# A CTR tower with two CIN layers: remainder from gathered rows, near product in halves, another order of TensorE's passes

## The reference

```python
def _cin_layer(h, h0, W, b):                       # h: (B, Hn, 64), h0: (B, 32, 64)
    Wr = W.reshape(W.shape[0], Hn, Mn)
    x = jnp.einsum('bhd,bmd,ohm->bod', h, h0, Wr) + b[None, :, None]
    return jax.nn.relu(x)
x1 = _cin_layer(h0, h0, W1, b1)                    # 128 rows out of 32 x 32 pairs
next_hidden, direct1 = x1[:, :64], x1[:, 64:]
direct2 = _cin_layer(next_hidden, h0, W2, b2)      # 128 rows out of 64 x 32 pairs
z = jnp.sum(jnp.concatenate([direct1, direct2], axis=1), axis=-1)   # 192 per sample
y = relu(relu([z, dense_ctx] @ W_top1 + b_top1) @ W_top2 + b_top2) @ W_top3
```

## Time and profile before

| | |
|---|---|
| median of three runs | 2034.1 us |
| profiled execution | 2035.26 us, its span 2033.5 us |
| mean granted TensorE clock | 0.997 |
| PE busy | 1999.9 us (98%), 7038 instructions |
| PEld busy | 1325.8 us (65%) |
| DVE busy | 1923.5 us (95%) |
| ACT busy | 1713.6 us (84%) |
| POOL busy | 1647.3 us (81%) |
| DMA | 474.16 MB, mean 233 GB/s |

### The profile page before, as it was taken

How to read it: one execution, slowest core, us unless ns; L and a number is a source line. 1 busy time by engine, 2 the same in 40 slices (tenths; PEclk the granted TensorE clock), 3 DMA queues, 4 the chain that set the end, 5 groups by cost and what they waited for, 6 DMA issues and landing times.

```text
span 2033.5 us, 24093 instructions
## 1 busy us (share of the span) xinstructions
PE 1999.9 (98%) x7038; PEld 1325.8 (65%) x7038; DVE 1923.5 (95%) x546; ACT 1713.6 (84%) x4887; POOL 1647.3 (81%) x708
## 2 busy tenths in 40 slices
PE   5999999999999999999999999999999999999999
PEld 3666666666666666666666666666666666666664
DVE  6999999999999999999999999999999999999991
ACT  4788888888888888888888888888888888888873
POOL 5898887879899998887889998788999988887520
PEclk9999999999999999999999999999999999999999
DMA  7898988988988989989989989989988989989950
GB/s 227 217 268 235 245 246 232 245 248 232 245 249 234 248 244 235 250 241 236 253 237 237 254 237 236 257 232 237 257 233 238 255 231 239 255 230 238 251 131 11
DMA packets 257782, 474.16 MB, mean 233 GB/s; under 512 B 35425, under 2 KB 52321, under 8 KB 257522
## 3 DMA queue, kind: packets, MB, share of 16 engines
q1 hardware_dynamic: 230450, 396.18, 64.5%
q0 software_dynamic: 26624, 75.52, 22.0%
q10 hardware_dynamic: 576, 0.92, 0.1%
HBM read 321.49 MB, written 16.78 MB: 166 GB/s over the span
## 4 chain that ended last, share of the span: by engine, by line
PE 90%; DMA 3%; DVE 2%; ACT 2%; issue 2%; POOL 1%; SPq 0%; DVEq 0%; POOLq 0%; ACTq 0%
PE acc L592 20%; PE acc L604 17%; PE acc L605 17%; PE acc L610 17%; PE acc L615 14%; DMA plo<-pnear 2%; DVE pnear L514 2%; PE acc L595 1%; ACT phi L789 1%; ACT x L713 1%; POOL prod L308 1%; DMA x1rep<-x 1%; PE x1p L686 0%; DMA near<-emb_rows 0%; PE acc L686 0%
## 5 line engine op out<-in xcount | busy, mean ns | idle before, releaser
L271 POOL DMA_INDIRECT gathered<-in_tables,idx x256 | 655.4, 2560 | 101.8 <-POOL idx L266 51.2
L308 POOL TENSOR_TENSOR prod<-near,h 128x2048 f32<-128x2048 f32 x126 | 582.5, 4623 | 128.5 <-PE acc L595 81.1
L604 PE MATMUL acc<-phi,w2lo 128*128 128x512 f32 x1664 | 655.2, 394 | 8.2 <-ACT phi L789 8.0
L605 PE MATMUL acc<-phi,w2hi 128*128 128x512 f32 x1664 | 654.3, 393 | 0.0
L514 DVE TENSOR_TENSOR pnear<-near,x1p 128x4096 f32<-128x4096 f32 x128 | 564.9, 4413 | 6.2 <-ACT x1p L762 3.8
L514 DVE TENSOR_TENSOR pfar<-far,x1p 128x4096 f32<-128x4096 f32 x128 | 564.9, 4413 | 0.7 <-PE acc L615 0.7
L592 PE MATMUL acc<-prod,w1T 128*128 128x512 f32 x1024 | 460.1, 592 | 1.5 <-DVE prod L489 1.5
L610 PE MATMUL acc<-plo,w2hi 128*128 128x512 f32 x1664 | 454.5, 423 | 0.0
L713 ACT ACTIVATE x<-acc,bias 128x64 f32<-128x64 f32 x1024 | 305.8, 324 | 170.6 <-PE acc L595 170.6
L519 DVE TENSOR_TENSOR plo<-pnear,phi 128x3072 fp32r<-128x3072 f32 x128 | 446.2, 3486 | 0.3 <-ACT phi L789 0.3
L519 DVE TENSOR_TENSOR plo<-pfar,phi 128x2560 fp32r<-128x2560 f32 x128 | 361.2, 2822 | 45.1 <-ACT phi L801 45.0
(11 more groups left out here) (75 smaller groups left out, 1151.3 us busy)
## 6 DMA issues: line engine op xcount, KB each, us to landing
far<-emb_rows SPq DMA_DIRECT2D x512, 256.0 KB, 4.6
near<-emb_rows SPq DMA_DIRECT2D x510, 256.0 KB
plo<-pnear POOLq DMA_DIRECT2D x128, 512.0 KB
x1rep<-x SPq DMA_DIRECT2D x255, 256.0 KB, 4.3
h<-emb_rows SPq DMA_DIRECT2D x128, 256.0 KB
emb_rows<-gathered SPq DMA_DIRECT2D x127, 128.0 KB
gathered<-in_tables,idx POOLq DMA_INDIRECT x256, 6.6
rem_a<-emb_rows SPq DMA_DIRECT2D x64, 64.0 KB
```

Of the source, the lines that this page charges most:

```text
L271: nc.gpsimd.indirect_dma_start(out=gathered[s][:, g, :], out_offset=None, in_=a["tables"], in_offset=bass.IndirectOffsetOnAxis(ap=idx[s][: ...
L308: nc.gpsimd.tensor_tensor(prod1[:, :, :], near[(u + 2) % 3][:, :, :], h0[odd][:, :].unsqueeze(1).to_broadcast([P, K1, N]), ALU.mult).then_ ...
L604: nc.tensor.matmul(acc2[s][:, :], w2lo[:, t, :], phi[:, t, :], start=(t == T_DMA), stop=False)
L605: mm = nc.tensor.matmul(acc2[s][:, :], w2hi[:, t, :], phi[:, t, :], start=False, stop=(t == T_SPLIT - 1))
```

## The change

- The remainder's factors no longer come from `emb_rows`. One is the lower half of the gathered rows as they lie, the other is the upper half, moved down 64 partitions by a DMA (`move_upper`). GpSimd multiplies 64 x 256 instead of 32 x 512. ScalarE rounds once (64 x 256), at the end of odd steps, instead of twice at the front of even ones. GpSimd's subtraction writes its own tile, and three DMAs of SyncE (`place_remainder`) put the parts in one of two `rem_parts`.
- The lookups read their indices from `idx_all` directly; `place_idx` is gone.
- `pnear` is made in two instructions of 4 tiles. ScalarE rounds tiles 2 and 3 after the first, tiles 4 to 7 after the second. The part of `plo` for the DMA has its own two buffers.
- ScalarE copies x1 to PSUM after L801's rounding, not ahead of it.
- TensorE's order in a step: `high` of 2 and 3, `high` of 4 to 7, `whole`, `high` of 0 and 1, the first layer of chunk c+2, `low` of 2 to 7, `low` of 0 and 1, `low` of 8 to 12, `high` of 8 to 12.
- For chunks 0 and 1 x1 is made in one instruction without sums (`early_x1`); the sums follow later. The first `pnear` reads the replicated x1 in SBUF. Four unused matmuls instead of eight run ahead of step 0.

```diff
-            def load_rem(col):
-                for t, f0 in ((rem_a, 0), (rem_b, HALF)):
-                    src = bass.AP(emb, f0 * ROW + col, [[ROW, HALF], [N, 2], [1, N]])
-                    sp.dma_start(t[:, :], src).then_inc(rem_in, 16)
+            def move_upper(pair, s):
+                if pair:
+                    sp.wait_ge(rem_prod_ready, pair)
+                sp.dma_start(rem_b[:, :, :], gathered[s][HALF * GS:F * GS, :, :]).then_inc(rem_b_in, 16)
+            def place_remainder(pair):
+                sp.wait_ge(rem_lo_ready, pair + 1)
+                if pair >= 2:
+                    sp.wait_ge(acc1_ready, 2 * pair - 2)
+                for b, part in enumerate((rem_hi, rem_hi, rem_lo)):
+                    home = rem_parts[pair % 2][b * REM:(b + 1) * REM, :].rearrange("r (w n) -> r w n", w=2)
+                    sp.dma_start(home.bitcast(fp32), part[:, :].bitcast(fp32)).then_inc(rem_in, 16)
...
             # SyncE, step
+                if not odd and within(at, 2):
+                    place_remainder(pair + 1)
...
+                    if odd:
+                        sp.wait_ge(emb_stored, STORES * (pair + 3))
                     load_near(sp, (c + 3) * N, 1 - odd, u % 3)
                 if not odd and within(at, 5):
                     store_rows(pair + 2, (u // 2 + 2) % 3, turn + (u // 2 + 2) // 3 + 1)
+                    move_upper(pair + 2, (u // 2 + 2) % 3)
...
             # DVE, step
                 if begun(at):
                     dve.wait_ge(lo_near_ready, c)
+                    dve.wait_ge(hi_dma_ready, c)
                     dve.wait_ge(lo_dma_in, 16 * c)
-                products2(pnear[:, :, :, :], near[u % 3][:, :, :], odd, K1).then_inc(pnear_ready, 1)
+                for a in range(A2):
+                    near_half(c, u, a).then_inc(pnear_ready, 1)
...
             # TensorE, step
-                pe.wait_ge(hi_near_ready, c + 1)
+                pe.wait_ge(hi_near_ready, 2 * c + 1)
                 if at is None or at >= 2:
                     pe.wait_ge(z2_ready, c - 1)
-                high(odd, range(T_DMA, T_NEAR))
+                high(odd, range(T_DMA, K1))
+                pe.wait_ge(hi_near_ready, 2 * c + 2)
+                high(odd, range(K1, T_NEAR)).then_inc(hi_near_used, 1)
+                pe.wait_ge(pfar_ready, c + 1)
+                whole(odd).then_inc(far_used, 1)
                 pe.wait_ge(hi_dma_ready, c + 1)
-                high(odd, range(0, T_DMA)).then_inc(hi_near_used, 1)
+                high(odd, range(0, T_DMA)).then_inc(hi_dma_used, 1)
                 if within(at, 2):
                     pe.wait_ge(p1_ready, c + 3)
-                    pe.wait_ge(rem_lo_ready, pair + 2)
+                    pe.wait_ge(rem_in, 48 * (pair + 2))
                     pe.wait_ge(z1_ready, c + 1)
-                    layer1(odd)
+                    layer1(odd, pair + 1)
...
-                pe.wait_ge(pfar_ready, c + 1)
-                whole(odd).then_inc(far_used, 1)
+                pe.wait_ge(lo_near_ready, c + 1)
+                low(odd, range(T_DMA, T_NEAR))
                 pe.wait_ge(lo_dma_in, 16 * c + 16)
                 low(odd, range(0, T_DMA)).then_inc(lo_dma_used, 1)
-                pe.wait_ge(lo_near_ready, c + 1)
-                low(odd, range(T_DMA, T_NEAR))
...
             # ScalarE, step
-                    layer1(c + 1, 1 - odd)
-                if not odd and within(at, 2):
-                    remainder_hi(pair + 1)
-                act.wait_ge(pnear_ready, c + 1)
+                    if at == 0:
+                        early_x1(1)
+                    else:
+                        layer1(c + 1, 1 - odd)
+                act.wait_ge(pnear_ready, 2 * c + 1)
...
+                nc.scalar.activation(plo_dma[odd][:, :, :], products[:, 0:T_DMA, :], ACT.Copy, scale=-1.0).then_inc(minus_ready, 1)
...
+                nc.scalar.copy(phi[:, T_DMA:K1, :], products[:, T_DMA:K1, :]).then_inc(hi_near_ready, 1)
+                act.wait_ge(pnear_ready, 2 * c + 2)
+                nc.scalar.copy(phi[:, K1:T_NEAR, :], products[:, K1:T_NEAR, :]).then_inc(hi_near_ready, 1)
...
                 nc.scalar.copy(phi[:, 0:T_DMA, :], products[:, 0:T_DMA, :]).then_inc(hi_dma_ready, 1)
+                act.wait_ge(pfar_ready, c + 1)
+                if begun(at):
+                    act.wait_ge(acc2_ready, c)
+                nc.scalar.copy(phi[:, T_NEAR:T_SPLIT, :], ...).then_inc(hi_far_ready, 1)
                 if within(at, 1):
                     act.wait_ge(x1rep_in, 16 * A2 * c + 32 * A2)
...
                     copy_x1rep(1 - odd)
-                act.wait_ge(pfar_ready, c + 1)
...
+                if at == 0:
+                    late_sums(1, 1)
+                if odd and within(at, 3):
+                    remainder_hi(pair + 2)
```

More of the change, by code:

```diff
@@ L66, in build_dlrm @@
         idx_all = sb("idx_all", [P, PAIR_GATHERS, PAIRS], i32)
-        idx = [sb(f"idx_{s}", [P, PAIR_GATHERS], i32) for s in range(3)]
+        lookups_mark = sb("lookups_mark", [1, 1])
         gathered = [sb(f"gathered_{s}", [P, PAIR_GATHERS, D]) for s in range(3)]
@@ L82, in build_dlrm @@
         far = [sb(f"far_{s}", [P, K2, N]) for s in range(2)]
[L83 to L86, removed]
+        rem_b = sb("rem_b", [HALF * GS, PAIR_GATHERS, D])
+        rem_prod = sb("rem_prod", [HALF * GS, PAIR_GATHERS * D])
+        rem_hi = sb("rem_hi", [HALF * GS, PAIR_GATHERS * D], fp32r)
+        rem_lo = sb("rem_lo", [HALF * GS, PAIR_GATHERS * D], fp32r)
+        rem_parts = [sb(f"rem_parts_{s}", [3 * REM, N], fp32r) for s in range(2)]
         prod1 = sb("prod1", [P, K1, N])
@@ L92, in build_dlrm @@
         phi = sb("phi", [P, T_SPLIT, N], fp32r)
-        plo = sb("plo", [P, T_SPLIT, N], fp32r)
+        plo = sb("plo", [P, T_SPLIT - T_DMA, N], fp32r)
+        plo_dma = [sb(f"plo_dma_{s}", [P, T_DMA, N], fp32r) for s in range(2)]
         sums1 = sb("sums1", [P, B])
@@ L284, in low_parts @@
                 pool.sem_inc(lo_begun, 1)
-                nc.gpsimd.dma_start(plo[:, 0:T_DMA, :], pnear[:, 0, 0:T_DMA, :], accum_op=ALU.add
+                nc.gpsimd.dma_start(plo_dma[c % 2][:, :, :], pnear[:, 0, 0:T_DMA, :], accum_op=ALU.add
                                     ).then_inc(lo_dma_in, 16)
[L288 to L291, removed]
             def remainder_low(pair):
                 pool.wait_ge(rem_hi_ready, pair + 1)
-                nc.gpsimd.tensor_tensor(rem_parts[2 * REM:3 * REM, :], rem_prod[:, :],
-                                        rem_parts[0:REM, :].bitcast(fp32), ALU.subtract).then_inc(rem_lo_ready, 1)
+                nc.gpsimd.tensor_tensor(rem_lo[:, :], rem_prod[:, :], rem_hi[:, :].bitcast(fp32),
+                                        ALU.subtract).then_inc(rem_lo_ready, 1)
             def step(c, turn, u, at):
                 pair, odd = turn * (U // 2) + u // 2, u % 2
[L300 to L303, removed]
+                if not odd and begun(at) and within(at, 2):
+                    remainder_low(pair + 1)
                 if within(at, 2):
@@ L312, in step @@
                 if odd and within(at, 3):
[L313 to L318, removed]
+                    remainder_products(pair + 2, (u // 2 + 2) % 3)
                 if within(at, 7 - odd):
@@ L324, in step @@
                         pool.wait_ge(emb_stored, STORES * pair + STORES)
-                        place_idx(pair + 3, u // 2)
+                        pool.wait_ge(rem_prod_ready, pair + 1)
                     for g in range(2 * odd, 2 * odd + 2):
-                        gather(g, u // 2)
-            remainder_products(1)
+                        gather(g, pair + 3, u // 2)
+            for pair in range(2):
+                for g in range(PAIR_GATHERS):
+                    gather(g, pair, pair)
+                if pair == 0:
+                    nc.gpsimd.memset(lookups_mark[:, :], 0.0).then_inc(lookups_begun, 1)
+            remainder_products(0, 0)
+            for g in range(2):
+                gather(g, 2, 2)
+            remainder_low(0)
+            for g in range(2, PAIR_GATHERS):
+                gather(g, 2, 2)
+            remainder_products(1, 1)
+            remainder_low(1)
             all_steps(step)
@@ L362, in _ @@
             store_copy(sp, 0, 0, 0)
+            move_upper(0, 0)
             sp.wait_ge(emb_stored, STORES)
@@ L411, in step @@
                     load_far((c + 2) * N, odd)
[L412 to L417, removed]
                 if at == 3:
@@ L609, in low @@
                 for t in parts:
-                    mm = nc.tensor.matmul(acc2[s][:, :], w2hi[:, t, :], plo[:, t, :], start=False, stop=False)
+                    part = plo_dma[s][:, t, :] if t < T_DMA else plo[:, t - T_DMA, :]
+                    mm = nc.tensor.matmul(acc2[s][:, :], w2hi[:, t, :], part, start=False, stop=False)
                 return mm
@@ L726, in remainder_hi @@
                 act.wait_ge(rem_prod_ready, pair + 1)
```

(5 more changed lines are left out.)

109 lines of the change are left out of this document (59 added, 50 removed).

## The result

The changed kernel takes 2068.9 us, the median of four runs (2067.1 to 2072.0), against 2033.7 before (also four runs): ratio 1.0173, interval [1.0157, 1.0189]. I had forecast 2060, within 2038 to 2084.

The account below looks back on a forecast made before the run. TensorE was taken as the bound, with 90% of the chain. The terms 39.7 - 3.4 - 3.3 - 7.5 = +25.5 us on the profiled 2035.3 gave 2060.8, less 1.2 for the median: 2060 us, range 2038 to 2084.

Parts of the forecast that it names:

- The loop through ScalarE: Every middle step: TensorE's first pass on tile 4 waits 0.32 us for ScalarE's second rounding; +39.7 us over 124 steps.
- E: The end of the remainder pass on TensorE, from which the prediction counts times within a step.
- A pass ends 0.56 us after ScalarE: TensorE's waits: a pass that waits for ScalarE ends 0.56 us after ScalarE does, its weight load starting only then.
- Rival 3: At TensorE's wait for ScalarE: the weight load runs ahead, so the stall is 0.21 us; 2046 us, chance 0.06.
- The other engines at no cost: Middle steps: extra work on DVE, SyncE, GpSimd and DMA stays hidden; cost nothing, bounds -2 and +15 for remainder and lookups.
- My 0.5 us of room: Middle steps, worse half: the adding DMA lands 0.5 us before `pnear` must start for `pfar` to be in time.
- Old stalls of 3.4 us gone: Middle: the old stalls between remainder passes are mostly covered by the longer step; -3.4 us, bounds -3.4 and 0.
- The start: Up to step 1's remainder pass: earlier adding DMA and a shorter way from its landing; -3.3 us, bounds 0 and -8.
- The end: Last chunk: `pnear` begins sooner and fewer passes follow `pfar`; -7.5 us, bounds -4 and -8.
- the second gain: Last chunk: eight passes run beside `pfar`, then `whole` and four passes; 12.4 us instead of 17.5, 5.1 less.
- From span to median: Whole kernel: the median of the runs was taken to lie 1.2 us below the profiled execution, 2060.8 us.

Follow-up runs that it names:

- x1: The changed kernel with `whole` put back behind the first layer: 2019.9 us, ratio to before 0.9927.
- x2: The changed kernel with only the four `high` passes of tiles 0 and 1 moved behind the first layer: 2021.4 us, 0.9937.
- x4: The changed kernel with ScalarE rounding tiles 0 and 1 ahead of tiles 4 to 7: 2187.8 us, 1.0753.
- x5: The kernel before with one edit, `whole` ahead of the passes of tiles 0 and 1 and of the first layer: 2264.9 us, one run.
- x3: The changed kernel with ScalarE's negative copy behind its second rounding instead of ahead of the first: 2149.3 us, 1.0566.
- x6: x1 with ScalarE's copy of x1 to PSUM ahead of the rounding of tiles 8 to 12: 2021.6 us, 0.9934.
- x9: x8 with the adding DMA of step 0 issued ahead of `prod1` of chunk 2: 2017.0 us, 0.9911.
- x11: x1 with x1 of chunks 0 and 1 made in eight pieces with their sums again: 2022.5 us, 0.9942.
- x10: x1 with the edits of x6 and x7 together: 2028.7 us, 0.997.
- x7: x1 with `pnear` made in one instruction from step 1 on: 2025.9 us, 0.9949.
- x8: x1 with the near tiles of chunk 2 loaded without waiting for x1 of chunk 0: 2018.2 us, 0.9914.

## Why the prediction was right, and where its sizes were off

*The loop through ScalarE.* This was right: the place of the wait, who releases it, and that the loop closes. Worked out: ScalarE done at E + 6.19, the pass on tile 4 due at 6.43, late by 0.32. Measured: 1009.22 + 1.97 - 1004.98 = 6.21, due at 6.42, late by 0.35, and 0.36 per period. The interpolated rounding of 2048 elements, 1.91, is 1.952 in the mean; the two shorter instructions ahead of it are 0.01 to 0.02 below what I took, so that the errors cancel in part. An error of 0.04 in a difference of two sums near 6 makes 5.1 us in 124 steps (44.8 for 39.7); old stalls of 3.8 for 3.4 take 0.4 off. The 4.7 left are half of what the forecast lacked. x1 and x2 remove the wait by cover alone, x4 makes it longer by what it puts into the loop, and x5 by the cover that it takes away. One reading of the kernel before was too generous: I called ScalarE 0.5 us early there. By the rule of 0.56 the first pass of an even step ends at E + 7.36 + 0.56 = 7.92 and is due at 7.86 + 0.23 = 8.09, so the room was 0.17 us.

*A pass ends 0.56 us after ScalarE.* 1011.75 - 1011.19 = 0.56 again, and the weight load again starts only with the wait's end, 0.05 us behind the end of L831 in all 128 steps. That weight loads are pulled ahead of running matmuls, as the Trainium skill says (TensorE: Matmul & The Clock Gate, section "Step-by-step: what each phase is for"), is not seen across a semaphore wait here. Rival 3 falls.

*The other engines at no cost.* This was right: no wait ahead of `whole` for `pfar` in the changed kernel beyond 0.8 us in all, and steps of 15.18 in x2, where `whole` asks for it as early. DVE did wait for the adding DMA in 56 steps, without TensorE being touched. My 0.5 us of room, worked out for the worse half of the steps, was too small for most: `pnear` began 12.6 us behind E in the median step, not 12.9 to 14.3, and `pfar` was done 2.3 us before the first pass of `whole` in the median, 0.75 in the tightest step. That this chain also closes on itself, and takes over when its DMA goes later, the prediction did not see; x3 shows it.

*Old stalls of 3.4 us gone.* This was right: in x1, x2, x6 to x9 and x11 all periods lie within 0.08 us of the median. With the copy and the undivided `pnear` together (x10) 0.8 us come back; what set the old ones off each time was not tried.

*The start.* -1.75 for -3.3. The near tiles landed at 43.2, not at 41.8, and the DMA took 7.9: `pnear` of step 1 began at 55.9 where I had 54.6. x11 prices the early x1 at 1.7; x7 prices the split at 3.4, 1.6 of it by the clock. Together they are more than the change as a whole gained there. Its order of passes gives part back: step 1 waits for `pfar` until 64.7, which x1 does not, and the fourth remainder pass of x1 comes 2.3 sooner. The new wait for x1 ahead of the near tiles of chunk 2 costs another 1.2 (x8).

*The end.* -7.4 for -7.5: `pnear` of the last chunk comes 12.8 after E, `whole` 8.87 later, as worked out. The forecast compared two whole chains, and that was enough for the sum. It does not tell what one edit is worth, and my account of it as two gains that add was too simple. The place of `whole`, which I counted in the second gain, is worth 0.3 (66.2 us behind the last remainder pass in x1, 65.9 in the changed kernel). The copy and the split are worth 0.6 and 1.8 alone but 4.5 together, some 1.1 of it by the lower clock level.

*From span to median.* I subtracted 1.2 us, as the profiled run before lay above its median. The profiled run after is the lowest of its four, 1.8 below the median: 3.0 us of the some 9 by which the forecast was low.

## What to carry to other kernels

Where one engine is busy all the time, moving its own work is not free: each piece can be what hides another engine's chain. Follow the loops (last use here, the other engine's chain, first use there, and back), write down for each the time it takes once round, and compare it with the step. A loop that is longer by a third of a microsecond costs it in every step; a chain that is not closed costs once.

## What the runs showed that I had not expected

- The adding DMA is a loop of its own: 8.2 us to land, and 16.3 us round when its source is copied after both halves (x3).
- Two edits that cost 0.6 and 1.8 us at the end alone cost 4.5 together, as TensorE then idles 2.35 us, waits a second time, and has a granted clock of 0.60 on the mean of the next four microseconds (x10).
- A stall of 0.35 us in every step, 2% of the time, left the granted clock at 1.00 in the middle of the kernel (window 300 to 1650 us of the changed kernel):

```profile
300.00:1650.00 1350.00, 1344.71 (x4692) 876.61 (x4691) 1301.89 (x435) 1110.38 (x3349) 1022.42 (x435) 1.00 0.90 241
```

- Nor did 1.29 us in every step of x4 lower it in the middle. In x5, with 2.40 and 1.18 us in turn, it fell to 0.50 six times, for 3.4 us and at a cost of 1.5 us each.
